# Rotary weights loaded and prepared in the expert stage, and the last additions and row statistics spread over the rotary stage's first tiles

## The reference

```
x = x + L0_attn(norm(x));   x = x + L0_xattn(norm(x), ctx);   x = x + L0_ffn(norm(x))
x = x + L1_attn(norm(x));   x = x + L1_xattn(norm(x), ctx);   x = x + L1_ffn(norm(x))
```

```
q = norm(x)*g_q + b_q @ Wq + bq;   kv = norm(x)*g_kv + b_kv @ Wkv + bkv
rr, ri = |x_row| * cos(t*f), |x_row| * sin(t*f)      # one number of the row scales all angles
q, k = layernorm_per_head(rotate(q)), layernorm_per_head(rotate(k))
out = softmax(q k^T / 4) v @ Wo + bo
```

## Time and profile before

| | |
|---|---|
| median of three runs | 1872.93 us (1871.71 to 1884.01) |
| the profiled execution, its own time | 1873.22 us |
| its span, first to last instruction | 1871.5 us |
| mean granted TensorE clock | 0.859 |
| busy share of the span | PE 78%, DVE 74%, ACT 57%, POOL 35% |
| rotary tiles, first `normalise` to last output addition | 1299.1 to 1499.3 us |

### The profile page before, as it was taken

The page is one execution under the profiler, slowest core; times in us unless marked ns, Lnnn a source line. Parts: engine busy times, 40 slices in busy tenths (PEclk is TensorE's granted clock), DMA queues, the critical chain, the costliest instruction groups (busy, mean ns, idle before and its releaser), DMA issues. The chain is left out here.

```text
span 1871.5 us, 40366 instructions
## 1 busy us (share of the span) xinstructions
PE 1467.8 (78%) x13805; PEld 930.2 (50%) x13820; DVE 1393.7 (74%) x2385; ACT 1068.7 (57%) x1820; POOL 652.1 (35%) x654
## 2 busy tenths in 40 slices
PE   1677776999999999999997466861687759956892
PEld 0455553444444444444447356761465547735782
DVE  6888874799999998888876773326789646667674
ACT  1777763777777776777763342431567435535461
POOL 1222212165555645454510254551333110027242
PEclk9655665999999999999998677985899779958896
DMA  6920000112212121212110153433000010024334
GB/s 157 332 104 1 1 1 33 37 34 56 60 46 69 46 67 49 63 53 64 52 26 2 40 159 121 136 109 109 1 1 0 1 26 1 0 87 135 100 106 157
DMA packets 93389, 123.67 MB, mean 66 GB/s; under 512 B 22945, under 2 KB 74217, under 8 KB 92867
## 3 DMA queue, kind: packets, MB, share of 16 engines
q1 hardware_dynamic: 83395, 98.88, 18.7%
q0 software_dynamic: 7776, 21.28, 3.2%
q10 hardware_dynamic: 2112, 2.10, 0.3%
HBM read 66.85 MB, written 40.30 MB: 57 GB/s over the span
## 5 line engine op out<-in xcount | busy, mean ns | idle before, releaser
L2643 DVE TENSOR_TENSOR lat_dsum<-lat_dsum,lat_Pb 125x896 f32<-125x896 f32 x320 | 481.5, 1505 | 43.0 <-ACT lat_Pb L2588 33.7
L2588 ACT ACTIVATE lat_Pb<-banks 125x896 f32<-125x896 f32 x384 | 329.2, 928 | 145.2 <-PE banks L2477 130.8
L2455 PE MATMUL banks<-lat_Pb,lat_kv 125*64 125x448 f32 x1536 | 306.5, 541 | 0.0
L2477 PE MATMUL banks<-lat_QH,lat_kT 64*125 64x448 f16 x1536 | 247.7, 363 | 5.0 <-DVE lat_QT L2613 2.1
L2477 PEld LDWEIGHTS banks<-lat_QH,lat_kT 64*125 64x125 f16 x1536 | 104.6, 133 | 139.3 <-issue 66.3
L2455 PEld LDWEIGHTS banks<-lat_Pb,lat_kv 125*64 125x64 f32 x1536 | 100.6, 137 | 146.4 <-issue 138.3
L2409 POOL TENSOR_TENSOR lat_kk<-lat_rot,lat_kk 125x768 f16<-125x768 f32 x32 | 66.9, 2090 | 265.3 <-ACT lat_kk L2547 265.3
L2978 POOL DMA_INDIRECT sent_outputs<-moe_yb,moe_yidx x98 | 99.4, 1014 | 135.9 <-ACT moe_yb L3235 107.7
L2477 PE MATMUL banks<-lat_QL,lat_kT 64*125 64x448 f16 x768 | 136.0, 351 | 0.0
L3116 PE MATMUL banks<-moe_w2d,moe_gT 88*128 (+3 forms) x780 | 106.1, 288 | 22.6 <-DVE moe_gT L3453 15.6
L3116 PEld LDWEIGHTS banks<-moe_w2d,moe_gT 88*128 88x128 f16 (+1 forms) x780 | 77.5, 103 | 39.6 <-issue 27.0
(11 more groups left out here) (446 smaller groups left out, 3256.8 us busy)
## 6 DMA issues: line engine op xcount, KB each, us to landing
moe_xb<-sent_rows SPq DMA_DIRECT2D x49, 257.0 KB
lat_raw<-in_ctx_dram SPq DMA_DIRECT2D x32, 375.0 KB
sent_rows<-zero SPq DMA_DIRECT2D x1, 7453.0 KB, 49.0
lat_QH<-lat_QT SPq DMA_DIRECT2D x64, 112.0 KB, 2.9
lat_QL<-lat_QT SPq DMA_DIRECT2D x64, 112.0 KB, 5.0
lat_rD<-lat_reciprocals SPq DMA_DIRECT2D x62, 112.0 KB, 2.8
moe_arena<-sent_outputs SPq DMA_DIRECT2D x12, 512.0 KB, 6.5
sent_rows<-zero SPq DMA_DIRECT2D x1, 5140.0 KB, 65.1
```

Source lines behind the costliest of these rows:

```text
L2455: ins = nc.tensor.matmul(ps[u * DC:(u + 1) * DC, 6, 0:8 * T], kv[:, par, tt, :], Pb[:, tile_slot(tt, par), u, :], start=tt == 0, stop=tt = ...
L2477: ins = nc.tensor.matmul(ps[0:KP, n % 3 * 2 + q, 0:8 * T], kT[rows, par, 2 * pair + low, 0:KP], Q[rows, par, 8 * u:8 * u + 8, :].rearrange ...
L2588: nc.scalar.activation(Pb[:, slot:slot + 2, u, :], ps[0:KP, n % 3 * 2:n % 3 * 2 + 2, 0:8 * T], ACT.Exp, scale=1.0 / QSCALE).then_inc(exp_d ...
L2643: ins = nc.vector.tensor_tensor(dsum[:, par], dsum[:, par], Pb[:, tile_slot(tt, par)], ALU.add)
```

## The change

Four edits.

1. A class `RotaryWeights` owns the rotary weights' tiles and their constants. They are allocated before moe0. Their loads (now 10, since `wo` takes two transfers in place of 16) are issued by SP at the head of moe0's main block. Their preparation on DVE, with the one PE product, stands at the end of moe0's main block.
2. SP loads only group 0 of `picked` (two transfers) in moe0's block. The other six are issued at the head of rot's block, and the 32 additions go there too.
3. `row_stats` is no longer called for rot, so its block is gone. The statistics are made in rot's main block in two parts: tiles 0 to 3 ahead of the tiles, and tiles 4 to 15 in pieces inside DVE's calls -2, -1 and 0. ACT makes the square roots of the second part in its calls -1 and 0, and takes one root of no use (`first_root`) first.
4. POOL fills the buffers and clears the old semaphores in rot's main block.

```diff
+class RotaryWeights:
+    NLOAD = 16 * (8 + 2)
...
+    def load(self, sp):
...
+        load(self.wqkv[:], t["rot_wqkv"].rearrange("(c p) n -> p c n", p=P))
+        load(self.bqk_raw[:], t["rot_bqkv"][0:2 * D].partition_broadcast(P))
...
+        for c in range(2):
+            load(self.wo[:, c, :],
+                 t["rot_wo"][256 * c:256 * c + 256, :].rearrange("(j r) d -> j r d", r=32)[:, 0:HD, :])
+
+    def project(self, nc, pe, Z):
+        pe.wait_ge(self.loaded, self.NLOAD)
+        pe.wait_ge(self.bvB_made, 1)
+        for c in range(2):
+            ins = nc.tensor.matmul(Z, self.bvB[:, c, :], self.wo[:, c, :], start=c == 0, stop=c == 1)
+        ins.then_inc(self.bvo_done, 1)
+
+    def prepare(self, nc, dve, hmask, Z):
...    (bvB, m4, bqk, sel3, b3, hgm and borow, the instructions that were L845 to L868)
@@ rot's main block
             def _(sp):
+                if rot:
+                    for q in range(1, 4):
+                        for c in range(2):
+                            load_picked(sp, k, picked, picked_in, q, c)
+                    for q in range(4):
+                        sp.wait_ge(picked_in[q], 32)
...
             def _(pool):
+                if rot:
+                    zero_buffers(pool)
+                    wipe_used(nc, k)
...
             def _(act):
+                if rot:
+                    nc.scalar.activation(first_root[:], hmask[:, 0:1], ACT.Sqrt)
...
+                def roots(h):
+                    act.wait_ge(var_made, 2 * h + 1)
+                    nc.scalar.activation(st_sd[:, 0, part], st["var"][:, part], ACT.Sqrt).then_inc(rooted, 1)
+                def norm_roots(h):
+                    act.wait_ge(var_made, 2 * h + 2)
...                  (two more roots)
                 def rotary(i, s4):
                     if live(i + 2):
                         keep_xT(i + 2)
+                    if isinstance(i, int) and i == 0:
+                        norm_roots(1)
...
                         keep_projected(i + 2)
+                    if isinstance(i, int) and i == -1:
+                        roots(1)
                     if live(i + 1):
                         keep_heads(i + 1)
...
             def _(dve):
+                def gather(first):
+                    tiles = range(first, first + 4)
+                    dve.wait_ge(picked_in[first // 4], 32)
+                    for c in range(2):
+                        for i in tiles:
+                            s(nc.vector.scalar_tensor_tensor(
+                                x[:, i, :], picked[:, c, i, :], cw[:, c, i:i + 1], x[:, i, :], ALU.mult,
+                                ALU.add))
+                        s.settle()
+                    for i in tiles:
+                        s(nc.vector.bn_stats(st_raw[:, i, :], x[:, i, :]))
...
+                    gather(0)
+                    row_variances(0)
+                    row_scales(0)
+                    head_scales(0)
+                    dve.wait_ge(prepared, 3)
...
                 def rotary(i, s4):
                     if live(i + 2):
                         normalise(i + 2)
+                    if isinstance(i, int) and i == -2:
+                        angles(0)
+                        gather(4)
+                    if isinstance(i, int) and i == -1:
+                        gather(8)
                     if live(i):
                         scale_heads(i)
+                    if isinstance(i, int) and i == 0:
+                        row_scales(1)
                     if live(i + 1):
                         heads(i + 1)
...
                         center(i)
+                    if isinstance(i, int) and i == -1:
+                        gather(12)
+                        row_variances(1)
+                    if isinstance(i, int) and i == 0:
+                        head_scales(1)
+                        angles(1)
@@ moe0's main block
             def _(sp):
+                if not gated:
+                    rotary.load(sp)
                 for e in range(RAW, NE):
                     load_raw(sp, e)
...
-                    for q in range(4):
-                        for c in range(2):
-                            load_picked(sp, k, picked, picked_in, q, c)
+                    for c in range(2):
+                        load_picked(sp, k, picked, picked_in, 0, c)
...
+                if not gated:
+                    rotary.project(nc, pe, ps[:, 6, 0:D])
...
-                (the 32 additions of all four groups)
+                if not gated:
+                    rotary.prepare(nc, dve, k["hmask"], ps[:, 6, 0:D])
```

More of the change, by code:

```diff
@@ L368, in float_attention @@
         yq, yT = sb("yq", [P, H, HD]), sb("yT", [P, 2, P])
[L369 to L374, removed]
+        rotary_weights = RotaryWeights.current if rot else None
+        if rot:
+            wo, loaded = rotary_weights.wo, rotary_weights.loaded
+        else:
+            wo, m4 = sb("wo", [P, 2, D]), sb("m4", [P, 4])
+            loaded, m4_made = sem("weights_loaded"), sem("masks_made")
+        own, own_pool, prepared, begun = (
+            sem("dve"), sem("pool"), sem("pads_zeroed"), sem("products_begun"))
         xn_made, xnT_done, xT_made, proj_done, v_made = (
@@ L461, in in_halves @@
             return w.rearrange("p (a q e) -> p q a e", a=2, q=2)
-        st = row_stats(nc, ctx, f"{kind}_stats", k, double=rot, load=load_weights, zero=zero_buffers)
+        if not rot:
+            st = row_stats(nc, ctx, f"{kind}_stats", k, load=load_weights, zero=zero_buffers)
         def row(buf, i):
@@ L650, in causal @@
                         keep_values(i + 2, (s4 + 2) % 4)
+                if rot:
+                    roots(0)
+                    norm_roots(0)
                 over_quads(act, rotary if rot else causal)
@@ L658, in _ @@
                 if rot:
[L659 to L664 removed]
+                    pe.wait_ge(rw.made, 1)
                 else:
@@ new lines, in row_variances @@
+                def row_variances(h):
+                    part = PARTS[h]
+                    var = st["var"][:, part]
+                    s.settle()
+                    for i in range(part.start, part.stop):
+                        s(nc.vector.bn_aggr(st_mv[:, i, :], st_raw[:, i, :]))
+                    s.settle()
+                    s(nc.vector.tensor_copy(st["mean"][:, part], st_mv[:, part, 0]))
+                    nc.vector.tensor_scalar(var, st_mv[:, part, 1], HEPS, None, ALU.add).then_inc(var_made, 1)
@@ new lines, in head_scales, with angles @@
+                def head_scales(h):
+                    part = PARTS[h]
+                    dve.wait_ge(rooted, 3 * h + 3)
+                    then(nc.vector.reciprocal(st_sd[:, 2, part], st_sd[:, 1, part]))
+                    then(nc.vector.tensor_tensor(st["rt"][:, part], st["r"][:, part], st_sd[:, 2, part],
+                                                 ALU.mult))
+                def angles(h):
+                    part = PARTS[h]
+                    n = part.stop - part.start
+                    hnorm = st["hnorm"][:, part].unsqueeze(2)
@@ L882, in _ @@
+                    dve.wait_ge(ms_made, h + 1)
+                dve.wait_ge(loaded, NLOAD)
+                if rot:
+                    gather(0)
[3 more added lines that the diff above has]
+                    dve.wait_ge(prepared, 3)
+                else:
+                    dve.wait_ge(prepared, 2)
+                    then(nc.vector.tensor_tensor(m4[:], hmask[:, 0:4], hmask[:, 4:8], ALU.add))
                     then(nc.vector.tensor_copy(idb[:], id32[:]))
```

193 lines of the change are left out of this document (106 added, 87 removed).

## The result

| | before | changed |
|---|---|---|
| median, same chip, 4 runs each | 1872.32 us (1869.42 to 1884.01) | 1852.09 us (1848.56 to 1853.94) |
| ratio, 95% interval | | 0.9884 [0.9843, 0.9926] |
| the profiled execution, its span | 1873.22, 1871.5 us | 1853.46, 1851.7 us |
| mean granted TensorE clock | 0.859 | 0.862 |
| busy share PE, DVE, ACT, POOL | 78, 74, 57, 35% | 79, 74, 58, 35% |

The changed kernel is 1.16% faster, between 0.74 and 1.57.

The account below looks back on a forecast made before the run. DVE was taken to bound the seam between moe0 and rot. A gain of 25.4 us less 6.1, 1.9 and 1.6 saves 15.8, giving 1857.4 us (0.84% faster), range 1851 to 1866.

Parts of the forecast that it names:

- what bounds the seam: Between moe0 and rot, nearly all the time is DVE's: busy 14.58 of 20 us between 1280 and 1300 us.
- the head start: DVE's path from the first landing of expert outputs to `normalise(0)` takes 7.7 us in place of 33.66, 25.9 us earlier.
- the cover named: The 6.0 us of rotary constants go to DVE's idle stretch from 1253.09, beside SP's wait for the output stores.
- Part 2: From `normalise(0)` to `scale_heads(0)`, DVE's moved work gives back 6.1 us: 16.1 us less what gaps hide.
- Part 4: In the first tiles, DVE's additions and other instructions slow beside POOL's work: 1.6 us lost, bounds 0 and 3.
- the 0.6 set as the mark: Additions above 0.6 us on average in the changed profile would make the prediction wrong at that step.
- Part 3: In call 0, `row_scales(1)`, ACT's two roots, `head_scales(1)` and `angles(1)` cost net 1.9 us after the waits they cover.
- 0.5 stood for the stores: At moe0's end, `prepare` on DVE beside POOL's last four indirect stores delays group 0 by 0.5 us, bounds 0 and 1.7.
- The first rival: No DVE contention, no POOL slip, ACT's roots unfelt in seam and first tiles: 19.6 us saved, 1853.6 us; chance 0.23.
- the case held likeliest: The whole kernel's time lies within 1% (18.7 us) of no change; chance 0.73.
- The third rival: TensorE's clock stays low in rot's tiles, each costing 2.4 us more: 1881 to 1891 us; chance 0.06, shared with an unshrunk seam.
- the second's table loads: One or two 1.28 us ACT table loads among the moved roots, in the dearer case of 1862.6 us; chance 0.11.

## Why the prediction was right or wrong

**Right: what bounds the seam, and the head start.** A to N gained 26.0, 26.3, 26.2 and 26.1 us for 25.9 predicted, `normalise(0)` came 7.62 us after the first addition (7.7), and the constants (1249.68 to 1255.67) were over before SP passed its wait. That they lay in DVE's idle stretch was the cover named. The first `scale_heads` came 21.9 us earlier (19 predicted), 19 without the 2.8 of scatter.

**Right: what comes back in calls -2 and -1.** 5.85, 5.2, 6.5 and 6.2 us against Part 2's 6.1, with the forecast order, L1031 at 1283.10 (1284.6 predicted) and no idle time before it. In the first profile POOL's share of this stretch nearly cancels (1.06 us paid, 0.99 given back), so Part 2 by itself was 5.8.

**The step that failed: Part 4, POOL beside DVE, put at a cost of 1.6 us, was nothing or a small gain.** It priced what the new order pays and what falls away from the old one from one kind of row, did not set the one against the other, and took about the middle of 0 and 3 (which would be 1.5). The two sides cancel. What the new order pays in the first profile: 3.85 - 3.37 and 3.95 - 3.37 on the two gathers beside POOL, and L1074's 0.60 in place of 0.19, 1.5 us in all. What the old order paid, in rows of the kernel before that the prediction did not list one by one:

```profile
1309.18 1.04 DVE L918 TENSOR_TENSOR rot_qk<-rot_qk,rot_rt 128x512 f32<-128x512 f32 x1
...
1316.67 0.71 DVE L940 SCALAR_TENSOR_TENSOR rot_hn<-rot_hn,rot_half_var 128x32 f32<-128x32 f32 x1
...
1317.64 1.10 DVE L944 TENSOR_TENSOR rot_qk<-rot_qk,rot_hm 128x512 f32<-128x512 f32 x1
```

After, these are 0.69, 0.19 and 0.69, and L907's 1.33 is 0.69: 0.35 + 0.52 + 0.41 + 0.64 = 1.9 us are given back. Net, the new order is 0.45 better. The prediction said that part of the 1.9 falls away; all of it did. In the four other profiles of the changed kernel the third gather took 4.43 to 4.50 us and not 3.95, so there the net is about nothing. In all four profiles of the kernel before, L918, L940 and L944 took the same 1.04, 0.71 and 1.10. The two runs with POOL's idle work show the mechanism: only POOL's reading instructions cost, 0.33 us each, and the fills do not. POOL is busy 652.1 and 652.3 us in the two kernels; what changed is which of DVE's instructions lie beside its own. The average addition of the third gather was 0.49 us, and 0.56 in the other profiles, below the 0.6 set as the mark.

**Part 3, call 0, was 1.2 and not 1.9.** `row_scales(1)` took 0.96 us (1296.23 to 1297.19) and cost nothing: from L899 to L907 of that tile it had been 1.29 us with the wait, and it was 0.33 without. `head_scales(1)` and `angles(1)` took 1.36 (1305.33 to 1306.69) and covered 0.35 (from `normalise` to `scale_heads` 0.68 before, 0.33 after); ACT's roots lengthened one wait from 1.30 to 1.51, 0.2 and not 0.4. Against it, t1 to t3 took 0.9 us longer, where nothing was forecast: DVE's waits for the square were still 1.31 and 0.86 in tiles 2 and 3 (0.70 and 0.69 before). It is no fixed price of the new order: the two versions with early first additions run the same calls, and in two of their three profiles t1 to t3 took 21.1 us, as in the kernel before. Its cause stays open.

Put together, what comes back after `normalise(0)` was 7.4, 6.65, 8.1 and 7.6 us in four pairs, and not 6.1 + 1.9 + 1.6 = 9.6. In the first pair it is 5.8 for Part 2, 1.2 for Part 3, -0.45 for Part 4 and 0.9 unforeseen. Ahead of the first addition 0.3 to 0.75 us were lost, where 0.5 stood for the stores. The sum is 17.6 to 19.4 for the seam, against 15.8. The first rival, more is hidden, named this direction and put it at 19.6 with 0.23. Its contention was nothing, as it said, but of the 1.3 us that it gives back besides (a term that it works out nowhere) at most 0.45 came; it had ACT's roots at 0 where they cost 0.2, and the stores did slip.

Of the 5.3 us between forecast and median, 3.9 are in the profiled execution (1853.46): 2.1 from the seam, 2.8 of scatter ahead of it, less 0.9 around it; the median lies another 1.4 below that execution. So Part 4 alone does not carry the result over 1%: with it at 0 or -0.45 the sum saves 17.4 to 17.9 us, 0.93 to 0.95%, still the case held likeliest. The rest is scatter, as far as the profiles show.

**Right for the wrong reason: the first addition.** It was expected near 1265.9, 6.1 us after SP's pass at 1259.83, and came 6.3 after SP's pass. The prediction held that the block passes while group 0 is on its way. In fact the block was last, by some 1.5 us over the data. The step behind it, that groups 1 to 3 start about 1 us later than before, was off by more: SP too could issue them only after the block had changed, at about 1263.6 and so 6.2 us after its pass. It cost nothing, since the second gather was due at 1272.27 and had no wait. The drain was in the trace of before, from 1255.9 to 1265.8; it was not read, because nothing waited for it there.

**The stores.** Four indirect stores beside DVE's constants took 0.96, 0.96, 1.21 and 0.96 us. Over the five profiles of the changed kernel they took 0.25 to 1.04 us more than four times 0.96, and no store over 1.48; in all four profiles of the kernel before each of the last four took 0.96. The 0.5 us for a slip was fair. The 3100 ns of the Trainium skill, "SBUF — State Buffer", section "A bandwidth-pool intuition that's wrong", were not seen. By that section a held store waits until the VectorE instruction ends, and no copy or cast beside these stores was longer than 0.51 us; the 0.52 us by which the longest store was stretched agrees with that, though no run here takes the copies away.

**The clock and the loads.** PE had a granted clock of 0.50 into the seam and again from 1290 to 1305, 0.84 from 1305 to 1310, 0.71 and 0.68 in the stretches from 1310 and from 1320 to 1325, and 1.00 from 1330 to 1341; tiles then came every 10.6 us. The third rival did not come. Nor did the second's table loads: ACT loaded a table at 1263.62, when it had nothing else to do, and again only for the first exponential.

## What to carry to other kernels

When work is moved out from behind a block's end, list what each engine does at that end, drains too, even where nobody waited for it: what was covered by a wait for data and 13.6 us of additions is next in line once they are gone. Then look for the next engine behind it: with the drain out of the way, SP's issues and DVE held the block, and 0.5 us was won in place of 1.0 to 1.6. Contention counts both ways; read every instruction that is slow in the old order, since moving work can also free it. And compare kernels by marks close to the edit, because two profiled spans of the same kernel here differed by up to 30 us from chip to chip and their starts of one stage by 11.

## What the hardware showed that was not expected

- POOL's drain at a block's end finished 7.4 us after its last indirect store in both kernels at moe0's end (1258.34 to 1265.8, 1255.93 to 1263.3) and 6.0 us after it at moe1's end (1822.35 to 1828.3), while SP saw the data landed 1.5 and 1.65 us after it. Other engines' drains took 0.01 to 2.5 us. What the drain waits for was not tried.
- A DVE addition with two inputs in SBUF is held up beside a POOL instruction that reads SBUF, by 0.33 us for each 0.73 us long instruction here, and not at all beside one that only writes.
